# Differential attention's TensorE work on four column tiles of 32: keys, values, causal mask, output product and the transposition of the tokens

## The reference, cut to what matters

```python
q = (x @ Wq).reshape(B, S, 2, h, dh); k = (x @ Wk).reshape(B, S, 2, h, dh); v = (x @ Wv).reshape(B, S, 2, h, dh)
s1 = jnp.where(causal, jnp.einsum('bshd,bthd->bhst', q1, k1) * scale, neg_inf)
s2 = jnp.where(causal, jnp.einsum('bshd,bthd->bhst', q2, k2) * scale, neg_inf)
a1, a2 = jax.nn.softmax(s1, axis=-1), jax.nn.softmax(s2, axis=-1)
o = einsum(a1, v1) - lam * einsum(a2, v2)
o = o.reshape(B, S, h * dh) * (1.0 - LAMBDA_INIT)
return o @ Wo
```

## Time and profile before

| | us |
|---|---|
| median of 3 runs (1642.93 to 1644.7) | 1644.26 |
| span of the profiled execution | 1642.7 |
| of it, TensorE busy with matmuls | 1577.1 (96%) |
| two pairs, one iteration of the loop | 39.58 |
| pairs in the phase | 32 |

### The profile page before, as it was taken

One profiled execution on the slowest core, in us unless ns is written; L12 is line 12 of the kernel. 1 busy time (PEld: TensorE's weight loads), 2 busy tenths in 40 slices (PEclk: granted clock), 3 DMA queues, 4 the chain that ended last, 5 costly groups with the idle time before them and its releaser, 6 DMA issues. The chain is left out here.

```text
span 1642.7 us, 51985 instructions
## 1 busy us (share of the span) xinstructions
PE 1577.1 (96%) x18084; PEld 1321.5 (80%) x18084; DVE 1227.7 (75%) x3513; ACT 914.9 (56%) x2620; POOL 676.4 (41%) x1068
## 2 busy tenths in 40 slices
PE   7999999999999999999999999899999999999795
PEld 5887788787777777777777777699999999999664
DVE  6889888677776777777777677478888888888664
ACT  5777777643544445544444545566666666666251
POOL 3666665411233333333333333234444444444345
PEclk9999999999999999999999999999999999999997
DMA  3214212121221000000001010122122122122231
GB/s 98 74 44 120 72 56 58 44 58 46 61 58 27 26 26 26 26 26 26 26 26 29 27 30 22 30 58 63 44 63 61 43 63 61 44 63 59 77 116 32
DMA packets 157654, 82.30 MB, mean 50 GB/s; under 512 B 17641, under 2 KB 153115, under 8 KB 157568
## 3 DMA queue, kind: packets, MB, share of 16 engines
q1 hardware_dynamic: 154800, 77.68, 17.7%
q0 software_dynamic: 2048, 3.15, 0.6%
q10 hardware_dynamic: 720, 0.33, 0.1%
HBM read 61.03 MB, written 21.27 MB: 50 GB/s over the span
## 5 line engine op out<-in xcount | busy, mean ns | idle before, releaser
L1489 PE MATMUL bank<-diff_xT,diff_w_score 128*128 128x128 f32 x2048 | 256.4, 278 | 0.7 <-ACT diff_xT L1606 0.7
L1489 PEld LDWEIGHTS bank<-diff_xT,diff_w_score 128*128 128x128 f32 x2048 | 238.7, 192 | 22.4 <-issue 20.2
L1613 ACT ACTIVATE diff_keys<-bank 128x512 f32<-128x512 f32 x256 | 152.3, 595 | 161.7 <-PE bank L1489 161.7
L2092 ACT ACTIVATE lat_prob<-bank,lat_neg_max 128x128 f32<-128x128 f32 x512 | 180.7, 367 | 89.9 <-DVE lat_neg_max L2247 89.4
L1803 POOL TENSOR_TENSOR diff_prob<-diff_prob,diff_inv_sum 128x512 f32<-128x512 f32 x64 | 67.1, 1049 | 369.4 <-DVE diff_inv_sum L1706 369.4
L2309 POOL TENSOR_TENSOR lat_prob<-lat_prob,lat_inv_sum 128x512 f32<-128x512 f32 x128 | 133.4, 1042 | 147.6 <-DVE lat_inv_sum L2229 146.6
L1983 PE MATMUL bank<-lat_catT,lat_w_score 128*128 128x128 f32 x1024 | 137.9, 278 | 3.2 <-issue 2.6
L2015 PE MATMUL bank<-lat_catT,lat_query 128*128 128x128 f32 x1024 | 138.7, 278 | 2.3 <-ACT lat_query L2103 2.1
L2003 PE MATMUL bank<-lat_w_vo,lat_ctxT 128*128 128x128 f32 x1024 | 130.3, 275 | 1.1 <-ACT lat_ctxT L2115 1.1
L1983 PEld LDWEIGHTS bank<-lat_catT,lat_w_score 128*128 128x128 f32 x1024 | 124.4, 192 | 4.8 <-issue 3.9
L2015 PEld LDWEIGHTS bank<-lat_catT,lat_query 128*128 128x128 f32 x1024 | 124.5, 192 | 4.7 <-ACT lat_query L2103 3.7
(11 more groups left out here) (274 smaller groups left out, 3684.3 us busy)
## 6 DMA issues: line engine op xcount, KB each, us to landing
lat_c_rep<-cat SPq DMA_DIRECT2D x128, 128.0 KB
stage<-low_y SPq DMA_DIRECT2D x64, 64.0 KB, 1.6
diff_x_rep<-stage SPq DMA_DIRECT2D x128, 32.0 KB, 1.8
lat_c_t<-cat SPq DMA_DIRECT2D x32, 128.0 KB, 2.2
exp_w<-in_L_ffn_w_dram SPq DMA_DIRECT2D x16, 256.0 KB
expert_rows<-latw_zeros SPq DMA_DIRECT2D x4, 548.0 KB, 5.6
exp_rows<-expert_rows SPq DMA_DIRECT2D x8, 274.0 KB
low_x_t<-in_x_dram SPq DMA_DIRECT2D x32, 64.0 KB, 1.9
```

Of the source, the lines that this page charges most:

```text
L1489: last = nc.tensor.matmul(ring[(k + d) % 2][:, j * P:(j + 1) * P], w_score[:, H1 * (k // 2) + HS * d + 4 * (k % 2) + j, :], xT[:, :], star ...
L1613: nc.scalar.activation(keys[:, k // 2, 4 * (k % 2):4 * (k % 2) + 4, :].rearrange("p h t -> p (h t)"), ring[(k + d) % 2][:, :], ACT.Copy).t ...
L2092: last = nc.scalar.activation(prob[:, q, m, :], ps_s[q][:, m * T:(m + 1) * T], ACT.Exp, bias=neg_max[:, q, m:m + 1], accum_out=row_sum[:, ...
```

## The change

Every matmul of the phase but `mixes` goes on four column tiles of 32, the form of `scores`. A new list `strips` holds the four slices of 32. Where one matmul with 128 stationary columns stood (keys, output product, mask, and the transposition, which becomes an f32 matmul with the identity), four with 32 stationary columns each stand now, one for each slice, writing 32 partitions of the same bank. `values`, which had two of 64 columns, has four of 32. The same columns stream through, and the same semaphores are raised, by the last of the four.

```diff
+        strips = [slice(32 * n, 32 * (n + 1)) for n in range(4)]
...
-                nc.tensor.transpose(ring[0][:, 0:P], x_t[:, :], core.ident[:, :]).then_inc(xt_done, 1)
+                for at in strips:
+                    last = nc.tensor.matmul(ring[0][at, 0:P], x_t[:, at], core.ident[:, :], start=True, stop=True)
+                last.then_inc(xt_done, 1)
...
-                    last = nc.tensor.matmul(ring[(k + d) % 2][:, j * P:(j + 1) * P],
-                                            w_score[:, H1 * (k // 2) + HS * d + 4 * (k % 2) + j, :], xT[:, :],
-                                            start=True, stop=True)
+                    for at in strips:
+                        last = nc.tensor.matmul(ring[(k + d) % 2][at, j * P:(j + 1) * P],
+                                                w_score[:, H1 * (k // 2) + HS * d + 4 * (k % 2) + j, at], xT[:, :],
+                                                start=True, stop=True)
...
-                        for par in range(2):
-                            w = wv[att][:, 4 * d + t, par * HD1:(par + 1) * HD1]
+                        for at in strips:
+                            par = at.start // HD1
...
-                nc.tensor.matmul(ps_hi[:, :].rearrange("p (h t) -> p h t", h=HS)[:, :, L:S], core.identb[:, :], mask,
-                                 start=False, stop=True).then_inc(s_done, 1)
+                for at in strips:
+                    last = nc.tensor.matmul(ps_hi[at, :].rearrange("p (h t) -> p h t", h=HS)[:, :, L:S], core.identb[:, at],
+                                            mask, start=False, stop=True)
+                last.then_inc(s_done, 1)
...
-                            last = nc.tensor.matmul(ring[1][:, 0:D], oT[:, t // 4, t % 4, :], wo[:, t, :],
-                                                    start=(t == 0), stop=(t == HS - 1))
+                            for at in strips:
+                                last = nc.tensor.matmul(ring[1][at, 0:D], oT[:, t // 4, t % 4, at], wo[:, t, :],
+                                                        start=(t == 0), stop=(t == HS - 1))
```

More of the change, by code:

```diff
@@ L1513, in values @@
                     for att in range(2):
-                        for par in range(2):
-                            w = wv[att][:, 4 * d + t, par * HD1:(par + 1) * HD1]
+                        for at in strips:
+                            par = at.start // HD1
                             tokens = mix[:, att:4 - att:3 - 2 * att, 2 * t + par, :, :].rearrange("p f b l -> p b f l")
                             last = nc.tensor.matmul(
-                                ring[d][par * HD1:(par + 1) * HD1, t * P:(t + 1) * P]
-                                .rearrange("p (b f l) -> p b f l", b=2, f=2),
-                                w, tokens, start=(att == 0), stop=(att == 1))
+                                ring[d][at, t * P:(t + 1) * P].rearrange("p (b f l) -> p b f l", b=2, f=2),
+                                wv[att][:, 4 * d + t, at], tokens, start=(att == 0), stop=(att == 1))
                 last.then_inc(o_done, 1)
@@ L1537, in scores @@
                 mask = tri[:, None, :].to_broadcast([P, HS, L])
-                nc.tensor.matmul(ps_hi[:, :].rearrange("p (h t) -> p h t", h=HS)[:, :, L:S], core.identb[:, :], mask,
-                                 start=False, stop=True).then_inc(s_done, 1)
-                nc.tensor.matmul(ps_lo[:, 0:LO].rearrange("p (h t) -> p h t", h=HS), core.identb[:, :], mask,
-                                 start=False, stop=True).then_inc(s_done, 1)
+                for at in strips:
[3 more added lines that the diff above has]
+                for at in strips:
+                    last = nc.tensor.matmul(ps_lo[at, 0:LO].rearrange("p (h t) -> p h t", h=HS), core.identb[:, at], mask,
+                                            start=False, stop=True)
+                last.then_inc(s_done, 1)
             def pair(i, par):
```

## The result

| | before | after |
|---|---|---|
| median | 1644.31 us | 1681.41 us (1680.48 to 1683.62) |
| after / before, 95% interval | | 1.0221 (1.0203 to 1.0240) |
| span of the profiled execution | 1642.7 us | 1680.3 us |
| packets on q8 | 52 | 192 |
| a pair without a jump, in the loop | 19.79 us | 19.08 us |

37 us slower. A pair is counted here from one start of the output product to the next. Both halves of the forecast are in the last two lines: pairs became 0.71 us shorter, and each of the 12 jumps back costs 4.89 us. 32 x 0.71 = 22.8 us won, 12 x 4.89 = 58.6 us lost: 35.9 of the 37.6 us between the two spans.

The account below looks back on a forecast made before the run. The prediction took TensorE's matmuls, one after another, to bound the changed phase. Seams, keys to values, rounds and transposition gave -14.9 us, loop code +27.6: +12.7 us on 1642.7, so 1657 us as median, range 1626 to 1670 us.

Parts of the forecast that it names:

- What bounds the kernel, and no more work per round: In the changed phase TensorE's matmuls one after another set the time; four column tiles give no more work per round.
- The seams, -13.4 us: Delays from values to scores and scores to mask go: 0.21 us in each of 64 half-steps, 13.4 us saved.
- Keys to values, -1.6 us: Half the delay between keys and values goes in one half-step: 0.05 us in 32 pairs; in the other a copy decides.
- Rounds and transposition, -3.4 + 3.5: Key and output product rounds take 0.109 instead of 0.111 us, 3.4 us saved; the transposition's second round adds 3.5 us.
- my sum of -14.9: Seams, keys to values, rounds and transposition together, before the code's cost: -14.9 us, from 0 to -22.
- What could be late next: VectorE's sum of the output product must precede the next pair's second key bank; said to fit still, by 0.3 us.
- Issue: Eight instructions per four-tile round at 13.6 ns each: taken as no cost; as rival bound 183 us more, chance 0.06.
- Code, +27.6 us: TensorE's loop body of 8.6 packets does not stay: 12 jumps back at 2.3 us, from 0 to 34; chance 0.74.
- The sign that I had named: In the changed profile, one TensorE gap of about 2 us behind the output product once an iteration, nothing else in it.
- The range: Forecast range for the whole kernel, 1626 to 1670 us, holding code that does not stay and code that stays, not issue.
- The rival "the loop's code stays": TensorE's jumps back are free if nine or more packets stay within reach: 1629 us, faster; chance 0.20.

Follow-up runs that it names:

- written-out form: The changed kernel with TensorE's loop of 13 iterations written out as 26 pairs of straight code, other engines keeping their loops: 1617.61 us, 0.9832 of before.
- the run with the head at place 0: The changed kernel with the first instruction of TensorE's loop at place 0 of a code packet, without announcement: 1694.18 us, 1.0275 of before.

## Why the prediction was right and wrong

**What bounds the kernel, and no more work per round:** right. The rounds of the output product went from 0.111 to 0.109 us, and between jumps the time is still TensorE's.

**The seams, -13.4 us:** right in mechanism, somewhat too small. A pair without a jump shows 0.51 us less at these four places (0.13 us each instead of the 0.10 and 0.11 that I gave), 16 us in 32 pairs.

**Keys to values, -1.6 us:** too small. In the half-step d = 1 the stretch from mixes to values shrank by 0.185 us, 5.9 us in all, because a seam into the whole array was longer than its one late start: 0.09 us late start of the values, as seen, and 0.095 us in the first key matmul behind the mixes, which I had not read as a seam at all (the earlier trace rows have both: from the keys at 795.69 to the values at 797.67 it is 1.98 us, from the output product at 801.34 to the keys at 803.12, as many rounds, 1.78). In d = 0 the stretch did not change (3.54 us before and after), as forecast, but for half another reason. I gave the 0.24 us between the third key copy's end and the values to the copy. Written out, the values start 0.06 us behind that copy:

```profile
809.81 0.60 ACT L1626 ACTIVATE diff_keys<-bank 128x512 f32<-128x512 f32 x1
810.47 0.43 PE L1526 MATMUL bank<-diff_mix,diff_raw_qkv 128*32 128x128 f32 x8
```

The remaining 0.18 us belongs to the loop's form; its waits go by register steps there and by constants in straight code, though I did not try the two apart.

**Rounds and transposition, -3.4 + 3.5:** the transposition cost what was forecast, 0.11 us a pair. The rounds saved half of what I gave: the output product went from 1.79 to 1.75 us up to the keys, the keys from 1.88 to 1.86 up to the mixes in d = 0 and not at all in d = 1. That is 0.05 us a pair or 1.7 us in all. All in all a pair won 0.71 us where my sum of -14.9 gives 0.47: 22.8 us, just beyond the -22 that I allowed.

**What could be late next:** nothing. VectorE's sum of the output product did not hold the second key bank.

**Issue:** no cost, as taken. The written-out form has no wait for issue in 460 us; its 64 records of keys take as long as in the loop.

**Code, +27.6 us: the step that failed, in size.** That 8.6 packets don't stay was right, and that this decides the sign was right. The price of a jump was 2.3 us, at most 2.85; it measured 4.89. Three parts were missing or small. The first stand is 3.1 to 3.6 us: from the branch to the next keys it takes 3.8 to 4.3 us, more than the 3.15 us that I put together from a packet's move and another queue's landing, and the 0.7 us of work still queued then (I gave 0.3) hide a part. I counted one packet, but the one behind it starts only 3.1 us after it, which makes a second stand of 0.8 to 1.4 us where the clock is full (the run with the head at place 0 takes it away). And I let the clock be: a stand of 3 us was followed by half clock at 8 of 12 jumps, which takes the place of the second stand and costs more: those pairs are 0.58 us longer than the others. The sign that I had named, one gap of about 2 us an iteration, did not hold: it was over 3 us, with a second stand or half clock behind it. With 4.89 us the sum would have been 1644.3 - 14.9 + 58.6 = 1688 us, and with the measured gain as well 1680 us, the measured time being 1681.

**The range** took its upper end from a jump of 2.85 us, although no row showed a jump that fetches. An upper bound made of pieces seen elsewhere is no bound on a chain that was never seen.

**The rival "the loop's code stays"** was the right picture of the rest: without jumps that cost, 1617.6 us, and some 1621 us (1644.3 - 22.8) in a loop that stays, against the 1629 us that I gave. It decided at fewer packets than my "nine or more": a loop must have under about seven.

## What to carry to other kernels

Before a change multiplies the instructions of a loop, count the body: on TensorE a loop of 1,670 instructions jumped back for free and one of 1,800 did not, and a jump then cost 2 to 5 us: the wait for the target's packet, and behind it a second wait or half clock. The 26 pairs in straight code cost nothing for their code here, so the cure is to write the loop out on that engine alone. Neighbouring matmuls in one array form save 0.1 to 0.2 us at each change of form, but a part that stays in another form brings back two changes: convert a chain as far as it goes. A branch announced to the sequencer helped only together with a place of the loop that puts the branch some 3 us behind its packet's beginning.

## What the chip showed that I had not expected

- The limit of a free loop on TensorE lies between 6.5 and 7.05 packets of 256 instructions; at 7.05 all packets come anew in each iteration (46 in 420 us for a body of 7.05 packets, nine in an iteration of 81 us).
- After a jump the next packet in sequence starts on q8 only 3.1 us behind the target's (675.8 and 679.0), 0.5 us after the first keys; in straight code there is no such stand.
- A stand of 3 us was followed by half clock for 3.4 us in the changed kernel at 8 of 12 jumps, and for 3.4 or 6.8 us with the loop's head elsewhere at 11 of 12, where the longer one cost 2.7 us a jump, nearly as much as the stand. After the stands of 1.5 to 2.2 us in the loops of six and four pairs it fell at 3 of 8 jumps.
- Entering the whole array from strips in f32 costs 0.2 us, one half of it in front of the first matmul and the other behind it.
